# Attention on one core: keys of the second query half in the order 0, 1, 4, 2, 5, 3, 6, 7, with a new table of ticks

## The reference, cut to what matters

```
mod = silu(c) @ wmod                        # six parts: sa, ca, ga, sb, cb, gb
h = layernorm(x) * (1 + ca) + sa
q, k, v = rope(h @ Wq), rope(h @ Wk), h @ Wv
att = q @ k.T / sqrt(32), causal
ctx = softmax(att) @ v
x = x + ga * (ctx @ Wo)
h = layernorm(x) * (1 + cb) + sb
x = x + gb * (h @ W.T + bias + lora(h))
```

## Time and profile before

| | |
|---|---|
| median of three runs | 2407.32 us |
| profiled execution, its own time | 2411.02 us |
| its span | 2409.2 us |
| mean granted TensorE clock | 0.992 |
| busy: TensorE / weight loads / VectorE / ScalarE / GpSimd | 98% / 68% / 73% / 42% / 65% |
| attention stage (560 to 1560 us): TensorE / VectorE / ScalarE / GpSimd | 991 / 940 / 636 / 879 us of 1000 |

### The profile page before, as it was taken

How to read it: one execution, slowest core, us unless ns; L and a number is a source line. 1 busy time by engine, 2 the same in 40 slices (tenths; PEclk the granted TensorE clock), 3 DMA queues, 4 the chain that set the end, 5 groups by cost and what they waited for, 6 DMA issues and landing times. The chain is left out here.

```text
span 2409.2 us, 37318 instructions
## 1 busy us (share of the span) xinstructions
PE 2349.1 (98%) x13260; PEld 1647.3 (68%) x13260; DVE 1764.7 (73%) x4224; ACT 1023.2 (42%) x1868; POOL 1577.9 (65%) x834
## 2 busy tenths in 40 slices
PE   5999999999999999999999999998999999999998
PEld 3788888888655555555555555544788888888886
DVE  4766667667999999999999999975545545555553
ACT  3433333331466666666666666775111111111111
POOL 3743334341698998999989999984654654654653
PEclk8999999999999999999999999999999999999999
DMA  6523333334355336334343345404323333333330
GB/s 239 200 88 115 121 120 118 123 110 122 92 165 154 85 88 175 83 83 134 77 103 86 86 138 124 103 19 151 110 93 104 107 94 99 111 95 96 113 89 27
DMA packets 179716, 267.22 MB, mean 111 GB/s; under 512 B 20508, under 2 KB 113884, under 8 KB 178400
## 3 DMA queue, kind: packets, MB, share of 16 engines
q1 hardware_dynamic: 179552, 265.13, 37.3%
HBM read 183.22 MB, written 80.81 MB: 110 GB/s over the span
## 5 line engine op out<-in xcount | busy, mean ns | idle before, releaser
L1101 POOL TENSOR_TENSOR p_sum<-p_sum,p_ring 128x768 f32<-128x768 f32 (+1 forms) x434 | 919.4, 2154 | 67.9 <-PE ctx_ps L1162 44.6
L995 ACT ACTIVATE p_ring<-scores 128x512 f32<-128x512 f32 (+1 forms) x896 | 444.3, 575 | 299.4 <-DVE scores L1049 224.3
L290 DVE CUSTOM_DVE_ANT_0 scores_q<-scores_q,mask_row 128x512 f32<-128x512 f32 x977 | 458.6, 514 | 33.8 <-PE scores_q L277 33.5
L277 PE MATMUL scores_q<-k_stack,q_stack 96*128 96x512 f32 (+1 forms) x1473 | 437.7, 372 | 6.6 <-DVE neg_max L290 6.0
L277 PEld LDWEIGHTS scores_q<-k_stack,q_stack 96*128 96x128 f32 x1473 | 252.9, 190 | 211.0 <-DVE neg_max L294 96.9
L1141 PE MATMUL scores<-q_stack,k_stack 98*128 98x512 f32 (+1 forms) x1216 | 371.7, 395 | 1.7 <-DVE neg_max L290 0.9
L646 POOL TENSOR_TENSOR roped_hilo<-roped_hilo 128x512 fp32r<-128x512 f32 x80 | 105.3, 1316 | 337.2 <-ACT roped_hilo L489 337.2
L294 DVE TENSOR_REDUCE neg_max<-scores_q 128x1 f32<-128x512 f32 x496 | 313.0, 684 | 3.6 <-PE scores_q L277 1.5
L695 PE MATMUL proj_ps<-h_hi,w_hi 128*128 128x512 f32 x752 | 297.8, 396 | 0.7 <-POOL w_lo L635 0.7
L695 PE MATMUL proj_ps<-h_hi,w_lo 128*128 128x512 f32 x752 | 293.6, 390 | 0.0
L695 PE MATMUL proj_ps<-h_lo,w_hi 128*128 128x512 f32 x752 | 293.2, 390 | 0.0
(11 more groups left out here) (169 smaller groups left out, 3657.2 us busy)
## 6 DMA issues: line engine op xcount, KB each, us to landing
q_stack<-qk_t SPq DMA_DIRECT2D x96, 512.0 KB, 6.9
qk_t<-roped_hilo SPq DMA_DIRECT2D x80, 512.0 KB, 2.8
x_in<-in_L_attn_resid SPq DMA_DIRECT2D x32, 512.0 KB, 6.3
ctx_t<-ctx_raw SPq DMA_DIRECT2D x64, 256.0 KB, 7.5
prefetched<-in_L_wmod SPq DMA_DIRECT2D x4, 4096.0 KB, 14.7
prefetched<-ctx_t SPq DMA_DIRECT2D x31, 512.0 KB, 4.1
prefetched<-inv_t SPq DMA_DIRECT2D x124, 128.0 KB, 5.4
k_stack<-qk_t SPq DMA_DIRECT2D x96, 128.0 KB, 8.7
```

Of the source, the lines that this page charges most:

```text
L277: last = nc.tensor.matmul(dst[:, a, :], qs[0:MHI, h, i * P:(i + 1) * P], ks[0:MHI, lo:lo + w], start=True, stop=True)
L290: last = nc.vector.tensor_tensor_reduce(src[:, a, :], src[:, a, :], sh.maskW[:, HALF - w:HALF], -1.0, LARGE, ALU.add, ALU.min, neg[:, a, :])
L995: nc.scalar.activation(p[:, a * per:(a + 1) * per, :], src[:, a * per:(a + 1) * per, :], ACT.Exp, scale=SM_SCALE).then_inc(s_ex.sem, 1)
L1101: nc.gpsimd.tensor_tensor(a, a, probs(n, u), ALU.add).then_inc(s_ap.sem, 1)
```

## The change

The key tiles of the second query half are taken in the order 0, 1, 4, 2, 5, 3, 6, 7. Key tiles 4 to 7 are those that meet the diagonal, so their masks no longer follow one on another: of half 1, units 10, 11, 14, 15, 18 and 19 carry masks, where 14 to 19 did before. The blocks are numbered in the new order (6 is key tile 4, 7 is 2, 8 is 5, 9 is 3). The flag that ends the accumulation follows the last block in place of key tile 3 or 7. The table `AFTER` is laid anew: the same 53 steps, with the maxima of the next group earlier at some units and later at others, and the values in other company. `SUM_AT_LAST` moves the last group's entry of half 1 from unit 6 to 5.

```diff
+KEY_ORDER = [(0, 1, 2, 3), (0, 1, 4, 2, 5, 3, 6, 7)]
 EXP_UNITS = []
 for _hf in range(2):
-    for _j in range(4 * _hf + 4):
+    for _j in KEY_ORDER[_hf]:
...
-QUADS = [[u for u in range(NE) if EXP_UNITS[u][:2] == k] for k in sorted(set(e[:2] for e in EXP_UNITS))]
+QUADS = [[u for u in range(NE) if EXP_UNITS[u][:2] == k] for k in dict.fromkeys(e[:2] for e in EXP_UNITS)]
...
-SUM_AT_LAST = {1: 6, 0: 12}
+SUM_AT_LAST = {1: 5, 0: 12}
...
 AFTER = [
+    maxima(1, 10),
+    maxima(1, 11, 12) + quads(-1, 10, 11),
+    maxima(1, 13, 14),
+    maxima(1, 15),
+    maxima(1, 16, 17) + quads(0, 0, 1) + maxima(1, 18, 19),
     [],
-    maxima(1, 10, 11, 12) + quads(-1, 10, 11) + maxima(1, 13, 14),
+    maxima(1, 20, 21) + quads(0, 2) + sums_of(-1, 1) + quads(0, 3) + maxima(1, 22),
+    maxima(1, 23, 24),
+    maxima(1, 25, 26),
+    maxima(1, 27) + quads(0, 4) + maxima(1, 28, 29),
     [],
-    maxima(1, 15) + quads(0, 0) + maxima(1, 16, 17),
+    maxima(1, 30, 31, 32) + quads(0, 5) + maxima(1, 33, 34),
+    maxima(1, 35),
+    maxima(1, 36, 37),
+    maxima(2, 0) + quads(0, 6) + sums_of(0, 0) + turned(1),
     [],
-    maxima(1, 18, 19) + quads(0, 1) + sums_of(-1, 1) + maxima(1, 20),
-    maxima(1, 21, 22),
-    maxima(1, 23) + quads(0, 2, 3) + maxima(1, 24, 25),
-    maxima(1, 26) + quads(0, 4) + maxima(1, 27, 28),
-    maxima(1, 29),
-    maxima(1, 30, 31),
-    maxima(1, 32, 33),
-    maxima(1, 34) + quads(0, 5) + maxima(1, 35),
-    maxima(1, 36, 37),
-    maxima(2, 0),
-    maxima(2, 1) + quads(0, 6, 7) + turned(1) + maxima(2, 2),
-    maxima(2, 3),
-    maxima(2, 4) + quads(0, 8) + maxima(2, 5, 6),
-    maxima(2, 7),
-    maxima(2, 8) + quads(0, 9) + sums_of(0, 0) + maxima(2, 9),
+    maxima(2, 1, 2, 3) + quads(0, 7) + maxima(2, 4),
+    maxima(2, 5),
+    maxima(2, 6, 7),
+    maxima(2, 8) + quads(0, 8, 9) + maxima(2, 9),
 ]
...
-                                                start=(j == 0), stop=(j == 4 * hf + 3))
+                                                start=(j == 0), stop=(q == LAST_QUAD[hf]))
```

## The result

The changed kernel takes 2416.71 us (median of 9 executions, 2414.46 to 2422.47); the kernel before, in as many, 2408.16 (2406.78 to 2412.88). The ratio is 1.0034, with a 95% interval of 1.0025 to 1.0043: slower, beyond the 0.2% that can be told here. The forecast was 2414.4, in a range of 2399 to 2421. The profiled execution took 2414.46 us with a span of 2412.7, 3.5 more than the span before, at the same mean granted clock of 0.992.

What follows compares the result with a forecast made beforehand. Three engines are nearly full, TensorE and VectorE tied by three PSUM banks and two score buffers. Per ordinary group -0.30 - 0.41 + 0.59 + 0.42 = +0.30 us; over 31 groups +7.1, so 2414.4 us, range 2399 to 2421.

Steps and rivals of the forecast that it cites:

- step 1: TensorE's visits to 32-column products: eight in place of nine per group, saving 0.30 us per group.
- step 2: TensorE's old waits at units 0 and 1, maxima 13 and 14, unit 11, maximum 19: all go, 0.41 us per group.
- step 3: New TensorE wait at unit 4 for unit 2's mask and exponentials: 0.59 us per group, bounds 0.3 to 0.75.
- step 5: What lies beside: ScalarE's waits, GpSimd's adds, the turn, DMAs: cost zero, with GpSimd's pause of about 1.4 us as cover.
- step 4: New TensorE waits for a bank at max 26 (0.12), 34 (0.14) and 37 (0.16): 0.42 us per group, from 0 to 0.6.
- step 6: The sum: an ordinary group +0.30 us; 27 such groups and four with a modulation product give +7.1 us in all.
- Modulation groups: Four of 31 groups: the product ahead of unit 4 hides its 0.59 us wait, so about -0.25 us each.
- the signs named as right: Groups of 31.4 us, unit 4 0.6 late, VectorE pauses 0.3 to 0.7 at max 22, 28, 1, share no higher, eight switches.
- (a): Rival: unit 2's exponentials are there when unit 4 comes, so the visit is won, 9.3 us, 2398; chance 0.22.
- Rival (b): Waits are only exchanged, old 0.41 and visit 0.30 against new 0.7 us: 2407; chance 0.15.
- Rival (c): VectorE's phase is worse, units 4, 16, 19 wait, unit 14's visit holds banks: +0.4 to 0.5 per group, 2422; chance 0.13.

Runs made afterwards that it cites:

- experiment 8: The changed kernel again, unedited, for the spread of one profile: 2415.43 us, 1.0023 of the kernel before.
- experiment 4: The changed kernel with blocks 0 and 1 in two visits, maximum 18 between them (nine visits): 2424.20 us, 1.0057 of the kernel before.
- experiment 3: The changed kernel without the causal mask on score unit 2: 2410.82 us, 1.0004 of the kernel before.
- experiment 9: The changed kernel with block 0 behind maximum 15 and ahead of unit 4, a ninth visit: 2416.76 us, 1.0023 of the kernel before.
- experiment 5: The changed kernel without the causal mask on score unit 11: 2407.70 us, 0.9991 of the kernel before.
- experiment 10: The kernel before, old key order, with a new eight-visit table, block 0 between units 3 and 4, blocks 3 and 4 apart: 2409.83 us, 0.9999.
- experiment 7: The changed kernel's new key order with another table of nine visits, block 0 between units 3 and 4: 2407.82 us, 0.9996 of the kernel before.
- experiment 11: The changed kernel's new key order, another nine-visit table with slack for GpSimd's adds ahead of the sums: 2412.96 us, 1.0009 of the kernel before.
- experiment 12: The changed kernel's new key order, a further nine-visit table without the slack for GpSimd: 2411.52 us, 1.0002 of the kernel before.

## Why the prediction was right

It forecast +7.1 us. The ratio gives +0.34% of 2408, 8.2 us, and the repeat in experiment 8 +5.6; the stage grew by 6.0. The mechanism is the forecast one: a visit is saved, and waits at unit 4 and for banks cost more than that. That the total comes so close is partly luck. 2.3 of the 6.0 us lie in the first group, of which the sum had nothing, and without them the stage is +3.7: an ordinary group lost 0.20 and not 0.30. The sizes below are means over the ordinary groups, place by place from the starts on TensorE.

- **Visits (step 1), right.** Eight, and 0.30 each: experiment 4 gave +0.28. The forecast set 0.30 from the rows against 0.11, an estimate from the Trainium skill (TensorE: Matmul & The Clock Gate, Single matmul latency). The measurement sides with the rows.
- **Old waits (step 2), undersized.** The step read 0.41 that would go, and all four places did lose their wait but for 0.02 at max 19. But more of the kind stood in the kernel before. All that its steps take above the price of their columns comes to about 1.1 us per group. Of this 0.34 is no wait: the four 128-column products of max 15 and of max 0 take 0.40 for 0.23 in both kernels, and their matmuls start 0.11 us apart, as far as their weight loads (1334.72, 1334.83, 1334.94 in the kernel before). Of the rest, some 0.75, 0.70 went. I had missed, for instance, 0.19 at unit 16 and 0.10 at max 3: in the timeline of TensorE before, the first 384-wide unit below takes 0.54 (1355.72 to 1356.26) and its repeat 0.35, and the maximum between them 0.28 for 0.18.
```profile
1355.72 0.52 PE L1141 MATMUL scores<-q_stack,k_stack 98*128 98x384 f32 x2
1356.26 0.44 PE L277 MATMUL scores_q<-k_stack,q_stack 96*128 96x384 f32 x1
1356.54 0.52 PE L1141 MATMUL scores<-q_stack,k_stack 98*128 98x384 f32 x2
1356.89 0.34 PE L277 MATMUL scores_q<-k_stack,q_stack 96*128 96x384 f32 x1
```
- **The wait at unit 4 (step 3), right in place and size, 0.61 for 0.59, and only half right in its cause.** It spreads over unit 3 (+0.12), max 15 (+0.24 over the 0.40 of before) and unit 4 (+0.25). The mask, the exponentials and the weight load follow each other as forecast. Unit 3's part is not of this chain: its second weight load is released by an exponential of unit 1. And experiment 3 shows a second feeder, ScalarE's own queue with the context copy, which step 3 did not have and step 5 put at nothing: without the mask 0.57 of the 0.61 is still there. That the mask's chain gave the size is luck in so far as the other is as long. Experiment 9 shows that position makes the wait.
- **Bank waits (step 4), undersized.** Max 26 has 0.10 (0.12 forecast), max 34 0.10 (0.14). Max 37 was to have 0.16; max 36, max 37 and unit 14 have 0.12, 0.11 and 0.05. Max 0 has 0.07 more than before. Together 0.55 for 0.42. Experiment 5 shows of the waits from max 34 to 37 that VectorE makes them; for max 26 and max 0 this is not shown.
- **The sum (step 6).** The period grew by 0.20 us. The saved visit and one shorter way out gave back 0.33 in place of 0.30, so waits grew by 0.53, net of what went, where the forecast had +0.60 (0.59 and 0.42, less 0.41). Two terms were undersized, the old waits (0.70 for 0.41) and the bank waits (0.55 for 0.42), and as they have opposite signs they partly cancelled. Added up place by place, 0.61 + 0.55 - 0.70 = 0.46; the other 0.07 lies in steps too small to be told apart. A group was to be 31.4 and is 31.33. In step 5 GpSimd's pause is 1.5 us by its rows, not 1.4; nothing hangs on it.
- **Modulation groups.** -0.25 forecast, -0.30 measured: the product ahead of unit 4 hides its wait. TensorE in such a group, with unit 4 at 0.57, the 0.10 behind 32-column products included:
```profile
918.24 3.66 PE L1209 MATMUL scores_q<-prefetched,silu_cols 128*32 128x256 f32 x64
921.83 0.72 PE L1142 MATMUL scores<-q_stack,k_stack 98*128 98x512 f32 x2
922.40 0.62 PE L278 MATMUL scores_q<-k_stack,q_stack 96*128 96x512 f32 x2
```
- **Not foreseen: the first group, +2.3 us.** TensorE in it stands still for 3.72 us ahead of unit 2, where the kernel before had 2.52 us, later: 1.2 us more. And 10.24 us are at half the clock where there were 6.83. They begin 1.02 us before the idle time ends, so 9.22 us of work are slowed and not 6.83, which costs an estimated 1.2 us (half of the difference). In experiment 8, the same kernel, they begin 2.47 us before it ends; the same sum gives 1.2 + 0.5 = 1.7 us, and the first group there is 1.7 longer than in the kernel before. The idle time does not decide how long the clock is low: experiment 10 has the same 3.72 us, but 6.83 us at half the clock, a clock of 0.91 from 620 to 660 us (0.87 in the changed kernel), and a first group of 36.04.
```profile
625.38 1.18 PE L1142 MATMUL scores<-q_stack,k_stack 98*128 98x384 f32 x2 [3.72 <-ACT p_sum L996]
```
- **What would show it.** The pauses of VectorE are 0.59, 0.31 and 0.34 where 0.3 to 0.7 was said; its share is 96.0% (96.3 before), the signs named as right. Of the rivals, (a) "the waits don't come" describes experiments 7 and 10, not the change. Rival (b), an even exchange, is what experiment 9 does at one place. Rival (c) had units 4, 16 and 19 wait; unit 16 has 0.04 and unit 19 nothing.

**What stays open.** In the traces, experiments 7 and 10 have a stage 5 to 6 us shorter than before, and their totals are the same as before within 0.1%. Over executions of one kernel, the total falls as the mean granted clock rises (correlation -0.8 to -0.94 in experiments 7 and 10 to 12, -0.5 to -0.8 in three sets of the kernel before; the ten executions of experiment 3 show none). The mean clock of all executions was 0.9905 in experiment 7 and 0.9913 in the kernel before beside it, 0.9895 in experiment 10 and 0.9911 beside it. A clock lower by 0.0016 of 2400 us is 3.8 us. Executions at the same granted clock show what the tables gained: at 0.990, experiment 10 takes 2407.6 us (mean of 4) and the kernel before 2412.5 (6); at 0.991, experiment 7 takes 2406.9 (7) and the kernel before 2409.7 (14). So the tables did gain 3 to 5 us at an equal clock, and most of what experiment 10 gained is lost in the clock. Why these kernels are granted less was not tried, and with one profile each it can't be placed. None of these kernels beats the kernel before outside its interval with all of the computation done.

## What to carry to other kernels

A merged visit is worth its switches only if what it pushes together was not holding something apart: here block 0 between units 3 and 4 was the time in which VectorE and ScalarE made the score buffer free. So list for each buffer the distance from its last writer to its next one, before and after, and price the shortest; and when all of one kind of wait is to be summed, take every step above its plain price, not those that look large, and set aside what is the same in every table, for it may be a price and no wait. For accumulators with one bank, keep other work between the last block of one half and the first of the next.

## What the runs showed of the hardware

- The switch to 32-column products and back has a price in three parts: 0.09 us ahead, 0.11 on the way out, 0.10 on the first matmul behind it, and 0.28 in the period of a group (experiment 4).
- A weight load follows the end of the exponentials it waits for by about 0.05 us (1337.99 to 1338.04), and then nothing hides it: unit 4's second matmul takes 0.34 (1338.04 to 1338.38) for 0.24.
- Four 128-column products with a weight load each start 0.11 us apart, as their weight loads do, and take 0.40 us together; their columns alone would take 0.23, as one maximum of 512 columns does (max 15 and max 0 in the kernel before).
- The granted clock also fell to half in the middle of the stage, for 3.41 us from 1164.7 us in experiment 11 and from 1161.3 in experiment 12. Both times TensorE had just stood still in group 16, where VectorE takes a reciprocal: for 0.93 us in two pieces until 1163.40 in experiment 11, for 1.47 us until 1160.01 in experiment 12. Group 16 took 34.18 and 33.94 us there, the other groups with a reciprocal 32.7. But the idle time does not decide alone: group 8 of the same two executions has the same idle time, and the clock stays at 1.00. The windows view of 1155 to 1170 us in experiment 11 shows the fall, as 0.89, with TensorE busy for 14.07 of 15 us; the same stretch is at 1.00 in the kernels before and after.
```profile
1155.00:1170.00 15.00, 14.07 (x71) 6.89 (x70) 13.17 (x46) 7.72 (x17) 15.00 (x7) 0.89 0.04 12
```
